# GpSimd's first eight row transfers of layer one, each behind a signal of TensorE

## The chip, the core and the metric

The kernel runs on one core of a Trainium2 chip. A core has TensorE (matrix products, written to PSUM), VectorE, ScalarE, GpSimd and SyncE, which run side by side and meet only at semaphores, and 16 DMA engines, which move data between HBM and the core's own memory. The metric is the device time of one execution in microseconds; less is better.

## The reference, cut to what matters

Three layers act on 4 sequences of 1,024 tokens with 128 features: a mixture of experts, a linear recurrence, and the same mixture of experts again. The two mixtures share their weights.

```python
x = x + 0.5 * ffn(layernorm(x))      # 8 experts, each token goes to 2 of them
x = x + lru(layernorm(x))            # complex diagonal recurrence along a sequence
x = x + 0.5 * ffn(layernorm(x))

def ffn(x):
    logits = x @ router_w.T + router_b
    topk_val, topk_idx = top_k(logits, 2)
    weights = softmax(topk_val)
    # every chosen expert: h1, h2 = split(x @ w1.T + b1); (silu(h1) * h2) @ w2.T + b2
    # the two results are summed with their weights
```

The reference computes all eight experts for all tokens and then picks. The kernel computes only what is picked.

## The kernel before, in words

**Routing.** A sequence g of a layer is 8 blocks of 128 tokens. VectorE and ScalarE normalise it, TensorE transposes it (`transpose_rows`, signal `s_tr`, one for each half) and multiplies it with the router's weights (`logits`, signal `s_logit`, one a sequence). VectorE picks the two best experts of each token (`choose`). TensorE then counts, by products with 0/1 matrices, how many tokens ahead of each chose the same expert (`rank`, signal `s_rank`, one a sequence), and from that VectorE makes the row of HBM to which each token goes (`slots`, signal `s_slot`). In the first layer the order of VectorE's work after the first sequence is written out by hand: slots of a sequence, the low half of a weight (`weight_low`), the low halves of the next sequence's rows (`row_parts`), `choose`, and so on.

**Rows.** GpSimd sends the tokens to their rows in HBM: `send_row(f, g, i)` is one indirect DMA of 128 rows, 16 of them for a sequence (8 blocks, two experts a token). In the first layer 42 of the 64 go ahead of all else on GpSimd (2 x 16 + `AHEAD_2`); the other 22 go two a tile within the first 11 tiles. The first of a sequence waits for `s_slot`, the ninth for `s_row`. In the kernel before, the seventh (`FIRST_PAUSE`) waits for the next sequence's logits too, and the thirteenth (`SECOND_PAUSE`) for its ranks.

**Experts.** The sorted rows are cut into 39 tiles of 256 rows (`NTILE`), each of one expert. When the last sequence's ranks and counts are there, VectorE makes a table of the tiles (`tile_table`), TensorE turns it into a row (`tile_row_of`, signal `s_listed`), and VectorE reads it back (`tile_list`, signal `s_tab`). SyncE then loads each tile, transposed, with its weights and biases (`load`). Tile 0 needs the 16 transfers of the first sequence, tile 1 those of the second, tile 9 of the third, tile 17 of the fourth (`FIRST_OF`, `s_sent`). TensorE starts on tile 0 when the weights of all eight experts are split into a high and a low half (`s_wl`); the last five splits stand behind `tile_list` on VectorE, and the loads of the experts 6 and 7 wait on SyncE for the splits of the experts 2 and 3, whose staging buffers they take. For a tile TensorE makes 24 products up (lines 1274 to 1276), and two tiles later two for the bias (line 1288) and 24 down (1294 to 1296). ScalarE and VectorE work between them. GpSimd scatters the two halves of each finished tile to HBM (`send_y`), and waits there for TensorE's products of three tiles on (`apart`).

The recurrence and the second mixture follow. The second layer's routing has pauses at the same two places.

Of the kernel before, what the change touches and what calls it, by code (L numbers as in the profile page):

```python
# [14 lines left out]
BATCH, SEQ = 4, 1024  # L15
# [21 lines left out]
STAGED = 4  # L37
AHEAD_2 = 10
FIRST_PAUSE, SECOND_PAUSE = 6, 12
APART = 3  # L40
LATE = BATCH - 1
RANKED, LISTED = 5, 10
# [12 lines left out]
def macaron_block(nc, x, nu_log, theta_log, b_re, b_im, c_re_t, c_im_t, d_vec, gamma_log,  # L55
                  router_t, router_b, w1_t, b1_t, w2_t, b2, out):
    ctx = ExitStack()
    with ctx:
# [3 lines left out]
        def sem(name):  # L62
            return ctx.enter_context(nc.semaphore(name))
# [133 lines left out]
        s_tr = sem("s_tr")  # L197
# [3 lines left out]
        s_logit = sem("s_logit")  # L201
# [4 lines left out]
        s_rank = sem("s_rank")  # L206
# [76 lines left out]
        def expert_tiles(f, tile):  # L283

            for t in range(NTILE):
                tile(t, lambda u: f * NTILE + t + u, lambda u, each: each * sent_before(f, t + u))
# [97 lines left out]
        @block.gpsimd  # L387
        def _(pool):
            pool.memset(ident[:, :], 0.0).then_inc(s_pool, 1)
            pool.memset(before[:, :], 1.0).then_inc(s_pool, 1)  # L390
            pool.iota(rev_i[:, 0:NE], pattern=[[-1, NE]], base=NE, channel_multiplier=0).then_inc(s_pool, 1)
            pool.iota(rev_i[:, NE:2 * NE], pattern=[[REG, NE]], base=0, channel_multiplier=0).then_inc(s_pool, 1)
            pool.iota(rev_i[:, 2 * NE:], pattern=[[1, 1]], base=0, channel_multiplier=1).then_inc(s_pool, 1)
            pool.iota(dest_i[:, :, :, :], pattern=[[TOK, TOPK], [SEQ, BATCH], [1, GT]], base=0,
                      channel_multiplier=GT).then_inc(s_pool, 1)
            pool.wait_ge(s_pool, 2)
            pool.affine_select(out=ident[:, :], in_=ident[:, :], compare_op=ALU.not_equal, fill=1.0, base=0,
                               pattern=[[-1, P]], channel_multiplier=1).then_inc(s_pool, 1)

            pool.affine_select(out=before[:, :], in_=before[:, :], compare_op=ALU.is_gt, fill=0.0, base=0,  # L400
                               pattern=[[1, P]], channel_multiplier=-1).then_inc(s_pool, 1)
            pool.memset(ones16[:, :], 1.0).then_inc(s_pool, 1)

            for m in range(TURNS):
                ins = pool.memset(double[:, m:m + 1], float(1 << m))
            ins.then_inc(s_pool, 1)

            def send_row(f, g, i):
                k, t = i // GT, i % GT
                if i == 0:  # L410
                    pool.wait_ge(s_slot, f * BATCH + g + 1)
                if i == GT:
                    pool.wait_ge(s_row, f * BATCH + g + 1)
                if i in (FIRST_PAUSE, SECOND_PAUSE) and g + 1 < (BATCH if f == 0 else LATE):

                    pool.wait_ge(s_logit if i == FIRST_PAUSE else s_rank, f * BATCH + g + 2)
                pool.indirect_dma_start(  # L417
                    out=rows_dram[f], out_offset=bass.IndirectOffsetOnAxis(ap=slot_i[:, k, f, g, t:t + 1], axis=0),
                    in_=rows[:, k, g, t, :], in_offset=None).then_inc(s_sent[g], 16)

            last_row = pool.to_reg(TOPK * TOK - 1)

            def apart(t, j, n):

                if t + APART < NTILE:
                    pool.wait_ge(s_up[j], n(APART + 1))

            def send_y(f, t, n):

                pool.wait_ge(s_yout, n(1))  # L430
                pool.sem_inc(s_ygo, 1)
                for r in range(2):
                    if r == 1:
                        apart(t, 0, n)
                    pool.indirect_dma_start(  # L435
                        out=y_dram[f],
                        out_offset=bass.IndirectOffsetOnAxis(ap=meta_i[:, t % METAS, r, 0:1], axis=0),
                        in_=yout[:, t % OUTS, r, :], in_offset=None, bounds_check=last_row,
                        oob_is_err=False).then_inc(s_ysent[t % OUTS], 16)

            for f in range(2):
                each = [(g, i) for g in range(BATCH) for i in range(TOPK * GT)]
                ahead = 2 * TOPK * GT + AHEAD_2
                for g, i in each[:ahead]:
                    send_row(f, g, i)
                later = iter(each[ahead:])

                def tile(t, n, dma):

                    send_y(f, t, n)  # L450
                    for j, (g, i) in enumerate(islice(later, 2 if f == 0 or t < 3 else BURSTS.get(t, 0))):
                        if j < 2:
                            apart(t, j + 1, n)
                        send_row(f, g, i)

                expert_tiles(f, tile)
# [933 lines left out]
```

## Time and profile before

| | us |
|---|---|
| median of 3 runs, no profiler | 562.7 (562.64 to 563.27) |
| profiled execution, first to last instruction | 662.6 |
| TensorE / VectorE / ScalarE / GpSimd busy in it | 481.3 / 425.0 / 350.1 / 284.6 |
| first product of tile 0, first product of tile 1 in it | 101.21, 105.60 |

The profile is one execution, with a record of every instruction. "Idle before <- X" in brackets is how long the engine had stood still before an instruction, and which one ended that. "Remote" and "issue" mean that the trace shows no instruction that ended it just then. The profiled execution shows no time of its own beside its span, and its span is 99.9 us above the median of the runs.

### The profile page before, as it was taken

What the parts mean: (1) busy time and instruction counts of PE and PEld (TensorE: products, weight loads), DVE (VectorE), ACT (ScalarE), POOL (GpSimd) and SP (SyncE); (2) the same over time, 40 slices, a digit from 0 to 9 for tenths busy, and PEclk for the clock granted to TensorE, in tenths of its full rate; (3) what the DMA queues carried; (4) which work ended last, traced back from release to release, by engine and by line L of the source; (5) the groups of instructions that cost most, each with busy time, mean ns of one, the idle gap of its engine ahead of it and who ended that gap; (6) DMA issues with size and microseconds to landing.
All of it is one profiled execution on the core that took longest, in us unless ns stands there. A gap on an engine that the chain in (4) does not pass through costs nothing.

```text
span 662.6 us, 15921 instructions
## 1 busy us (share of the span) xinstructions
PE 481.3 (73%) x4657; PEld 412.2 (62%) x4657; DVE 425.0 (64%) x1368; ACT 350.1 (53%) x797; POOL 284.6 (43%) x307
## 2 busy tenths in 40 slices
PE   7740008777699999998688777387945999999920
PEld 4530007556589899885587766266823998989920
DVE  8840387445478898772998772556823777767725
ACT  5871225445367777772506533075613677777820
POOL 1477600655655444453000574715465444444540
PEclk9555558987989999999697896679776999999975
DMA  8241132433223232204300111213222333333128
GB/s 288 73 145 48 48 104 43 89 84 74 66 58 73 63 57 59 63 27 142 114 0 1 34 46 36 65 34 76 54 78 77 71 68 68 60 62 61 46 72 309
DMA packets 94563, 50.27 MB, mean 76 GB/s; under 512 B 81902, under 2 KB 84720, under 8 KB 94484
## 3 DMA queue, kind: packets, MB, share of 16 engines
q1 hardware_dynamic: 85396, 32.31, 20.6%
q0 software_dynamic: 9088, 16.94, 8.1%
q8 instruction: 45, 0.74, 0.5%
q14 instruction: 34, 0.28, 0.2%
HBM read 17.25 MB, written 23.24 MB: 61 GB/s over the span
## 4 chain that ended last, share of the span: by engine, by line
PE 47%; issue 30%; DVE 9%; DMA 4%; ACT 4%; SPq 2%; another core or an unknown queue 1%; POOL 1%; POOLq 0%; DVEq 0%; ACTq 0%
PE bank L1276 10%; PE bank L1274 10%; PE bank L1275 10%; PE bank L1296 5%; PE bank L1294 5%; PE bank L1295 5%; DMA yin<-y 3%; PE bank L1288 1%; DVE w1l L825 1%; DVE xres L948 1%; ACT wst L551 1%; DVE wst L1063 1%; DVE bn L996 1%; ACT xn L472 1%
## 5 line engine op out<-in xcount | busy, mean ns | idle before, releaser
L435 POOL DMA_INDIRECT y<-yout,meta x156 | 154.0, 987 | 212.5 <-ACT yout L569 153.2
L1063 DVE SCALAR_TENSOR_TENSOR wst<-bank,bias,wst 128x256 f32<-128x256 f32 x312 | 146.5, 479 | 118.3 <-ACT wst L551 99.9
L1274 PE MATMUL bank<-xt_t,w1h 128*128 128x256 f16 x624 | 177.6, 285 | 27.2 <-DVE w2l L825 15.6
L417 POOL DMA_INDIRECT rows<-rows,slot_i x128 | 128.6, 1004 | 142.2 <-DVE slot_i L778 81.6
L551 ACT ACTIVATE wst<-bank,bias 128x256 f32<-128x256 f32 x312 | 141.5, 477 | 87.2 <-remote 64.2
L1276 PE MATMUL bank<-xt_t,w1l 128*128 128x256 f16 x624 | 177.3, 284 | 6.9 <-issue 6.9
L1275 PE MATMUL bank<-xt_t,w1h 128*128 128x256 f16 x624 | 177.4, 284 | 5.0 <-issue 5.0
L1294 PE MATMUL bank<-w2h,wst 128*128 x624 | 125.9, 224 | 8.1 <-issue 6.8
L1296 PE MATMUL bank<-w2h,wst 128*128 x624 | 124.0, 223 | 8.9 <-issue 8.8
L1295 PE MATMUL bank<-w2l,wst 128*128 x624 | 123.8, 223 | 6.9 <-issue 6.9
L1069 DVE TENSOR_TENSOR wst<-wst 128x512 f16<-128x512 f32 x156 | 107.6, 690 | 11.5 <-ACT wst L559 7.2
L559 ACT CAST wst<-wst 128x512 f16<-128x512 f32 x156 | 96.5, 619 | 29.2 <-DVE wst L1063 19.8
L1274 PEld LDWEIGHTS bank<-xt_t,w1h 128*128 x624 | 63.6, 102 | 35.3 <-issue 28.8
L1276 PEld LDWEIGHTS bank<-xt_t,w1l 128*128 x624 | 63.6, 102 | 18.8 <-issue 9.3
L1294 PEld LDWEIGHTS bank<-w2h,wst 128*128 128x128 f16 x624 | 62.2, 100 | 18.8 <-issue 14.5
L472 ACT ACTIVATE xn<-xres,shift,rstd 128x128 f32<-128x128 f32 x96 | 38.2, 481 | 64.3 <-DVE shift L711 42.1
L1275 PEld LDWEIGHTS bank<-xt_t,w1h 128*128 x624 | 63.5, 102 | 13.1 <-issue 8.0
L1295 PEld LDWEIGHTS bank<-w2l,wst 128*128 128x128 f16 x624 | 62.3, 100 | 11.3 <-issue 8.7
L1296 PEld LDWEIGHTS bank<-w2h,wst 128*128 128x128 f16 x624 | 62.4, 100 | 9.8 <-issue 9.6
L569 ACT ACTIVATE yout<-bank,meta 128x128 f32<-128x128 f32 x156 | 48.4, 363 | 28.3 <-remote 24.2
L948 DVE TENSOR_TENSOR xres<-xres,yin 128x1024 f32<-128x1024 f32 x16 | 19.6, 1224 | 27.8 <-DMA yin<-y 27.3
L1143 PE MATMUL bank<-ident,xn 128*128 128x128 f32 x96 | 20.3, 353 | 18.7 <-ACT xn L472 10.6
(205 smaller groups left out, 522.4 us busy)
## 6 DMA issues: line engine op xcount, KB each, us to landing
yin<-y SPq DMA_DIRECT2D x16, 512.0 KB, 4.6
wst<-in_w_t SPq DMA_DIRECT2D x8, 512.0 KB, 5.8
y<-yout,meta POOLq DMA_INDIRECT x156
rows<-padrow SPq DMA_DIRECT2D x18, 130.0 KB
xres<-in_x SPq DMA_DIRECT2D x8, 256.0 KB, 5.4
wst<-in_w_t SPq DMA_DIRECT2D x8, 256.0 KB, 6.8
rows<-rows,slot_i POOLq DMA_INDIRECT x128
out<-xres SPq DMA_DIRECT2D x4, 512.0 KB, 6.7
```

Of the source, the lines that this page charges most:

```text
L417: pool.indirect_dma_start(out=rows_dram[f], out_offset=bass.IndirectOffsetOnAxis(ap=slot_i[:, k, f, g, t:t + 1], axis=0), in_=rows[:, k, g ...
L435: pool.indirect_dma_start(out=y_dram[f], out_offset=bass.IndirectOffsetOnAxis(ap=meta_i[:, t % METAS, r, 0:1], axis=0), in_=yout[:, t % OU ...
L551: nc.scalar.activation(gate[:, j, :], up_ps[j][:, 0:SLOT], ACT.Silu, scale=1.0 / WS, bias=bias[:, t % STEP, j:j + 1]).then_inc(s_gate[j], 1)
L559: nc.scalar.copy(acth[:, t % BUFS, 2 * half:2 * half + 2, :], act[:, 2 * half:2 * half + 2, :]).then_inc(s_acth[half], 1)
L1063: V.scalar_tensor_tensor(act[:, j, :], up_ps[j][:, SLOT:], bias[:, t % STEP, HB + j:HB + j + 1], gate[:, j, :], ALU.add, ALU.mult).then_in ...
L1069: V.tensor_tensor(actl[:, t % BUFS, h2, :], act[:, h2, :], acth[:, t % BUFS, h2, :], ALU.subtract).then_inc(s_actl[half], 1)
L1274: T.matmul(o, w1h[:, bass.ds(at, P)], xt_t[:, t % STEP, 0, :], start=True, stop=False)
L1275: T.matmul(o, w1h[:, bass.ds(at, P)], xt_t[:, t % STEP, 1, :], start=False, stop=False)
L1276: ins = T.matmul(o, w1l[:, bass.ds(at, P)], xt_t[:, t % STEP, 0, :], start=False, stop=True)
L1294: T.matmul(o, acth[:, t % BUFS, c, rs], w2h[:, bass.ds(at, P)], start=False, stop=False)
L1295: T.matmul(o, acth[:, t % BUFS, c, rs], w2l[:, bass.ds(at, P)], start=False, stop=False)
L1296: ins = T.matmul(o, actl[:, t % BUFS, c, rs], w2h[:, bass.ds(at, P)], start=False, stop=(c == HB - 1 and r == 1))
```

## The change

In the first layer the pauses at the seventh and thirteenth transfer of a sequence go. In their place, transfers 1 to 8 of the first sequence (counted from 0) each wait for one further signal of TensorE, in the order in which it makes them: logits of sequence 1, transposes of 2, ranks of 1, logits of 2, transposes of 3, ranks of 2, logits of 3, ranks of 3. All later transfers of the first layer have only the waits for `s_slot` and `s_row`. The second layer keeps its two pauses.

```diff
+HELD = 8
...
-                if i in (FIRST_PAUSE, SECOND_PAUSE) and g + 1 < (BATCH if f == 0 else LATE):
+                if f == 0 and g == 0 and 0 < i <= HELD:
+
+                    turn, q = (i - 1) % 3, (i - 1) // 3
+                    if i == HELD:
+                        pool.wait_ge(s_rank, BATCH)
+                    elif turn == 0:
+                        pool.wait_ge(s_logit, q + 2)
+                    elif turn == 1:
+                        pool.wait_ge(s_tr, 2 * (q + 3))
+                    else:
+                        pool.wait_ge(s_rank, q + 2)
+                if f > 0 and i in (FIRST_PAUSE, SECOND_PAUSE) and g + 1 < LATE:
 
                     pool.wait_ge(s_logit if i == FIRST_PAUSE else s_rank, f * BATCH + g + 2)
```

## Rows read from the trace of the kernel before

**Rows 1.** The page's first line.
```profile
span 662.6 us, 15921 instructions
```

**Rows 2.** Windows, line 1288 alone (two products a tile): stretch, length, TensorE.
```profile
110.00:194.80 84.80, 4.02 (x27) 2.65 (x27) 0.90 0.33 73
203.00:292.00 89.00, 6.05 (x44) 4.02 (x44) 1.00 0.29 59
441.00:522.50 81.50, 3.47 (x23) 2.47 (x24) 0.81 0.28 68
```

**Rows 3.** Timeline of TensorE, routing and first tiles: start, length, operation.
```profile
41.77 3.56 PE L1156 MATMUL bank<-rwt,xnt 128*128 128x8 f32 x16
75.38 0.18 PE L1168 MATMUL bank<-seen,ones 128*128 128x32 f16 x1 [30.06 <-issue]
...
75.69 0.21 PE L1180 MATMUL bank<-seen,ones 128*128 128x64 f16 x1
...
101.21 0.39 PE L1274 MATMUL bank<-xt_t,w1h 128*128 128x256 f16 x1 [15.64 <-DVE w2l L825]
...
105.60 0.27 PE L1274 MATMUL bank<-xt_t,w1h 128*128 128x256 f16 x1
```

**Rows 4.** Timeline of VectorE, routing.
```profile
33.86 1.22 DVE L722 TENSOR_TENSOR rows<-xn,rows 128x1024 f16<-128x1024 f32 x1
37.96 0.23 DVE L737 TENSOR_TENSOR lg<-bank,rbb 128x64 f32<-128x64 f32 x1 [2.88 <-remote]
...
41.80 1.22 DVE L825 SCALAR_TENSOR_TENSOR w1l<-wst,w1h 128x1024 f16<-128x1024 f32 x1
...
48.72 0.23 DVE L768 TENSOR_TENSOR slotf<-bank,rev_f 128x64 f32<-128x64 f32 x1 [4.83 <-remote]
...
49.93 1.21 DVE L722 TENSOR_TENSOR rows<-xn,rows 128x1024 f16<-128x1024 f32 x1
71.35 0.23 DVE L737 TENSOR_TENSOR lg<-bank,rbb 128x64 f32<-128x64 f32 x1 [20.21 <-remote]
...
74.52 0.22 DVE L745 TENSOR_TENSOR oh<-oh 128x64 f16<-128x64 f32 x1
...
85.15 1.23 DVE L825 SCALAR_TENSOR_TENSOR w1l<-wst,w1h 128x1024 f16<-128x1024 f32 x1
```

**Rows 5.** Timeline of GpSimd: transfers 0, 8, 31 and 41.
```profile
24.22 1.86 POOL L417 DMA_INDIRECT rows<-rows,slot_i  x1 [21.55 <-DVE slot_i L778]
...
36.22 0.95 POOL L417 DMA_INDIRECT rows<-rows,slot_i  x1 [0.31 <-issue]
...
66.17 0.96 POOL L417 DMA_INDIRECT rows<-rows,slot_i  x1 [0.30 <-issue]
...
78.82 0.95 POOL L417 DMA_INDIRECT rows<-rows,slot_i  x1 [0.30 <-issue]
```

**Rows 6.** The chain of waits, last tiles: a scatter's issue and its landing.
```profile
637.69 0.98 POOL y L435
638.97 2.15 DMA y<-yout,meta
```

**Rows 7.** Timeline of SyncE and TensorE, second layer: tile 0's load, and its use.
```profile
419.04 1.27 SPq L344 DMA_TRANSPOSE xt_t<-rows  x1
...
422.18 0.39 PE L1274 MATMUL bank<-xt_t,w1h 128*128 128x256 f16 x1 [4.37 <-DMA xt_t<-rows]
```

**Rows 8.** Timeline of TensorE, second layer: tile 0's last products, tile 1's first.
```profile
426.73 0.27 PE L1276 MATMUL bank<-xt_t,w1l 128*128 128x256 f16 x1
432.29 1.11 PE L1143 MATMUL bank<-ident,xn 128*128 128x128 f32 x4 [5.29 <-issue]
...
435.17 0.42 PE L1275 MATMUL bank<-xt_t,w1h 128*128 128x256 f16 x1
```

**Rows 9.** Timeline of GpSimd, second layer: seventh transfer of a sequence, after its pause.
```profile
377.47 0.95 POOL L417 DMA_INDIRECT rows<-rows,slot_i  x1 [5.23 <-PE bank L1156]
```

**Rows 10.** Timeline of VectorE, second layer: the same signal, seen by VectorE.
```profile
377.22 0.23 DVE L737 TENSOR_TENSOR lg<-bank,rbb 128x64 f32<-128x64 f32 x1 [0.24 <-PE bank L1156]
```

## The prediction, made before the change was run

> **What bounds the kernel now.** I read the page first, for the span, and set it beside the median: the profiled execution takes 662.6 us [rows 1], the runs 562.7. So 99.9 us of the trace are not in the runs, and before a stall in it is priced one must ask whether the runs have it. Windows over the bias products come second, since they count tiles: in the quiet stretch of the first layer 22 tiles take 89.00 us, 4.05 each; in the stretch before it, where GpSimd makes four transfers a tile instead of two, 13.5 tiles take 84.80, which is 30.1 more than at 4.05; in the second layer 12 tiles take 81.50, 32.9 more [rows 2]. Most of each mixture is thus TensorE's own pace, and a start that is later or earlier by some us comes out at the end nearly one for one.
>
> The start is what the change touches, so the timelines of the routing are third. TensorE begins the last sequence's logits at 41.77 and is through at 45.33. VectorE, which waits for nothing else, takes them up at 71.35, after 20.21 idle, ended by "remote" [rows 3, 4]. It waited in the same way, for TensorE's signals, 2.88 before 37.96 and 4.83 before 48.72 [rows 4]. All that time GpSimd sends rows one after another [rows 5]. In the second layer, where GpSimd itself stands in a pause, a signal of the same kind ends VectorE's wait at 377.22 and GpSimd's at 377.47, both named after the product that gave it [rows 9, 10]. So in the trace TensorE's signals arrive late while GpSimd issues, and on time when it stands still. The three waits are 27.92 us of the start.
>
> **What the start would be without late signals.** The last ranks end at 75.69 + 0.21 = 75.90 [rows 3]; less the 27.92 that is **48.0**. The first product of tile 0 stands at 101.21 [rows 3]; less 27.92 that is 73.3. The tile table shrinks too: from the last pick (74.52) to the next weight split (85.15) VectorE takes 10.6 us for some 15 short links, while the pick, 14 such links, takes 74.52 - 71.35 = 3.2 [rows 4]. At that pace the table takes about 4.2, 6.4 less. TensorE could start at **66.9**. Tile 0's up products took 105.60 - 101.21 = 4.4 [rows 3], so tile 1 could start at 71.3 by the weights. Call D what of the late signals the runs do have: then it is 71.3 + D, with D = 34.3 in the trace.
>
> Tile 1 also needs transfer 31. It ends at 66.17 + 0.96 = 67.13 [rows 5]; a GpSimd scatter's landing ends 638.97 + 2.15 - 637.69 - 0.98 = 2.45 after its issue [rows 6]; a tile's load takes 422.18 - 419.04 = 3.14 until its first product [rows 7]. By the rows tile 1 can start at **72.7**. So tile 1 starts at the later of 72.7 and 71.3 + D. In the trace the second is far later (105.6) and the row transfers are hidden; without late signals the two are about level.
>
> **The change, part by part.**
>
> *The pauses taken away.* In the first layer they held nothing: the transfers stay at one per 1.265 us, which is (78.82 - 66.17) / 10, with 0.30 idle between them [rows 5]. Zero; the bounds are zero and some tenths, a register's worth of waiting each, under GpSimd's own 0.30.
>
> *The eight waits.* Seven of them end by the way, since the last ranks come after the signals that those wait for. The eighth decides: transfer 8, at 36.22 before [rows 5], cannot start until the last ranks, at 48.0 even when every signal is on time. That is **+11.8 us**, and behind it on GpSimd's queue stand transfers 9 to 41 and then the scatters of finished tiles, each moved by the same 11.8. Transfer 15, which tile 0 needs, ends at 48.0 + 7 x 1.265 + 0.96 = 57.8, lands at 60.3, and is loaded by 63.4: hidden behind the weights by 3.5 us, and if that cover went, tile 0 would wait. Transfer 31 is moved to 78.9 and tile 1 to **84.5**. Transfer 41 ends at 48.0 + 33 x 1.265 + 0.96 = 90.7; tile 0's scatter is due when tile 2 has its up products, some 6 us after 84.5, so it is hardly held. The 22 later transfers go with the scatters as before, 4 x 1.265 = 5.1 us a tile against 4.05 of TensorE, so that stretch gives nothing back.
>
> *TensorE's clock.* Between tile 0 (66.9 to 71.3, later by D) and tile 1 TensorE now stands still for up to 13 us. In the second layer it stood 5.29 us after tile 0 and its up products then took 0.42 again, after 0.27 [rows 8]. The lower level costs at most half of tile 0's 4.4, 2.2; below, nothing, if before pays it too. I take 1.5, nearer the top because the gap is longer than that of the row. Tile 1 counts as starting at 86.0.
>
> *What the waits buy.* When GpSimd stands still, signals arrive on time, so the held routing ends at 48.0 whatever D was. What they save is D, as far as it stood on the path.
>
> The change is then 86.0 less the later of 72.7 and 71.3 + D: +13.3 for D = 0, nothing at D = 14.7, and -19.6 with the trace's own 34.3.
>
> **How large D is in the runs.** In the trace's terms the start is late by 105.6 - 72.7 = 32.9, the busy stretches of the mixtures by 30.1 and 32.9: together 95.9. The runs lack 99.9. So nearly all of what the trace shows as late is missing from them, and if the second layer's routing has another 10 of it, about 10 are left for all places together. An even share leaves the start some 3; all of it at the start gives 10. I take D = 5, toward the middle because GpSimd is densest there. Change: 86.0 - 76.3 = **+9.7**, 562.7 + 9.7 = **572.4 us**. Its own range is D = 10 and no clock term (84.5 - 81.3 = +3.2) to D = 0 with all of it (86.7 - 72.7 = +14): 566 to 577. Against the profiled execution the same sum with its own D gives 662.6 - 19.6 = 643; I expect profile and runs to move in opposite directions.
>
> The Trainium skill bears on D (SBUF — State Buffer, section Who interferes with whom): TensorE never waits on another engine's use of the memory's ports. By that rule alone D would be 0 and the sum 576.0; the trace differs, its signals being late by up to 20.21 beside GpSimd's transfers [rows 4], and by it the sum would be 543. The page speaks of ports and not of signals, so it settles neither; the 572.4 does not use it.
>
> **Rivals.**
>
> *Faster: the signals are late in the runs as well.* The mechanism is the one above at its full size, at the start of layer one, where GpSimd issues 42 transfers with 0.30 between them. For it: it is in the trace, plainly, and the pauses of the second layer cure it there. Against it: 99.9 us that are not in the runs. It decides from D = 14.7; with D = 25 tile 1 was at 96.3 and comes to 86.0, so 562.7 - 10.3 = 552.4. Chance 0.28.
>
> *Slower still: the late signal moves on.* After 48.0 GpSimd sends 34 transfers freely, and the tile list's signal and tile 0's products fall beside them, where before they fell after 79.8, when it had stopped. The list's signal is queued ahead of five weight splits on VectorE. Were it late by 20.21, like the longest of before, TensorE would start at 87.1 and tile 1 at 91.5, with a warm clock: 91.5 - 76.3 = +15.2, 577.9. For it: nothing in the change pauses GpSimd there. Against: the same 99.9. Chance 0.10.
>
> *No change.* D is just about 14 and the later rows take up what the earlier list gives: 563. It needs a coincidence of two sums. Chance 0.06.
>
> **How the numbers follow.** The likeliest, 572.4, has 0.56; the other chances are as given. Slower by over 0.2% (1.1 us, about what a measurement of this kernel can tell from no change) is 0.56 + 0.10 = 0.66, within it 0.06, faster 0.28. A range of 552 to 578 leaves out the lower half of the faster case, a part of the slower rival and the upper edge of the likeliest, together near 0.2; the likeliest alone has 566 to 577.
>
> **What would show it.** Right: transfer 8 begins just after the last ranks, VectorE's three remote waits are gone or below 1 us, the last ranks end near 48, transfer 31 ends near 79, and tile 1's first product, not tile 0's, waits for its load at 84 or later. Wrong: transfer 8 earlier than 45 or later than 55 would break the +11.8; a late `s_listed`, seen as VectorE idle before `entry_i`, would be the third case; a median below 561.6 would show that the runs had D above 14.7, and that the subtraction of the two times, the weakest step, misled me.

## The result, and the profile after

The changed kernel takes 574.13 us (median of 4 runs, 572.33 to 575.82), the kernel before, run beside it, 562.99 (562.64 to 563.7). The ratio is 1.0196, its 95% interval 1.0165 to 1.0227: slower by 11.1 us, where +9.7 was forecast. (A ratio here is estimated from all the runs of both kernels, and can differ in the fourth place from the quotient of the two medians.)

The page's first line for the kernel after:

```profile
span 570.6 us, 15921 instructions
```

That is 3.5 us under the median of its runs, where the first trace of before stood 99.9 over its own [rows 1].

The timeline of GpSimd, kernel after: transfers 0, 7, 8, 16, 31 and 41.

```profile
24.18 1.85 POOL L429 DMA_INDIRECT rows<-rows,slot_i  x1 [21.51 <-DVE slot_i L790]
...
42.57 1.46 POOL L429 DMA_INDIRECT rows<-rows,slot_i  x1 [1.75 <-PE bank L1168]
48.45 0.96 POOL L429 DMA_INDIRECT rows<-rows,slot_i  x1 [4.42 <-PE bank L1192]
...
61.58 1.82 POOL L429 DMA_INDIRECT rows<-rows,slot_i  x1 [0.30 <-issue]
...
82.73 0.96 POOL L429 DMA_INDIRECT rows<-rows,slot_i  x1 [0.30 <-issue]
...
95.57 0.96 POOL L429 DMA_INDIRECT rows<-rows,slot_i  x1 [0.31 <-issue]
```

Against [rows 5], transfer 8 begins at 48.45 instead of 36.22, and what ended its wait is the product of the last ranks. Transfer 31 is at 82.73.

The timeline of TensorE, kernel after, which answers to [rows 3]:

```profile
38.73 3.56 PE L1168 MATMUL bank<-rwt,xnt 128*128 128x8 f32 x16
47.14 0.19 PE L1180 MATMUL bank<-seen,ones 128*128 128x32 f16 x1 [4.85 <-DVE seen L760]
...
47.44 0.21 PE L1192 MATMUL bank<-seen,ones 128*128 128x64 f16 x1
...
66.18 0.39 PE L1286 MATMUL bank<-xt_t,w1h 128*128 128x256 f16 x1 [15.71 <-DMA xt_t<-rows]
...
88.65 0.39 PE L1286 MATMUL bank<-xt_t,w1h 128*128 128x256 f16 x1 [18.24 <-DMA xt_t<-rows]
```

The ranks end at 47.65 (forecast 48.0), tile 0 starts at 66.18 (forecast 66.9, later by D), and then TensorE stands for 18.24 us until tile 1's rows are loaded.

The timeline of VectorE, kernel after, the places of [rows 4]:

```profile
34.96 0.22 DVE L749 TENSOR_TENSOR lg<-bank,rbb 128x64 f32<-128x64 f32 x1
...
40.78 0.22 DVE L780 TENSOR_TENSOR slotf<-bank,rev_f 128x64 f32<-128x64 f32 x1
...
43.12 0.21 DVE L749 TENSOR_TENSOR lg<-bank,rbb 128x64 f32<-128x64 f32 x1
...
46.27 0.22 DVE L757 TENSOR_TENSOR oh<-oh 128x64 f16<-128x64 f32 x1
...
50.05 1.23 DVE L837 SCALAR_TENSOR_TENSOR w1l<-wst,w1h 128x1024 f16<-128x1024 f32 x1
```

The three "remote" waits are gone, and the table from the pick to the next weight split takes 3.8 us instead of 10.6. Taken alone this is the trace of a cure. The first experiment shows that there was nothing to cure.

### The profile page after: what moved, and what is told of

Read it like the earlier page. It is cut to its first block, busy times and chain, and to the rows that moved or that the text cites. A ratio compares the mean times of both kernels' runs of the same rounds, so it can differ in the third digit from the quotient of the medians.

```text
span 570.6 us, 15921 instructions
## 1 busy us (share of the span) xinstructions
PE 449.6 (79%) x4657; PEld 394.9 (69%) x4657; DVE 424.1 (74%) x1368; ACT 358.1 (63%) x797; POOL 299.8 (53%) x307
## 4 chain that ended last, share of the span: by engine, by line
SPq 27%; PE 20%; DVE 17%; issue 12%; POOL 12%; DMA 8%; ACT 3%; POOLq 0%; ACTq 0%; DVEq 0%
SPq L345 10%; POOL rows L429 10%; SPq L355 4%; SPq L349 4%; PE bank L1286 4%; PE bank L1288 4%; PE bank L1287 4%; SPq L352 3%; SPq L336 3%; DMA yin<-y 3%; DMA xt_t<-rows 2%; DVE wst L1075 2%; PE bank L1307 2%; PE bank L1306 2%; PE bank L1308 2%
## 5 line engine op out<-in xcount | busy, mean ns | idle before, releaser
L447 POOL DMA_INDIRECT y<-yout,meta x156 | 161.2, 1033 | 116.3 <-ACT yout L581 81.5
L1286 PE MATMUL bank<-xt_t,w1h 128*128 128x256 f16 x624 | 173.6, 278 | 53.2 <-DMA xt_t<-rows 53.2
L429 POOL DMA_INDIRECT rows<-rows,slot_i x128 | 136.6, 1067 | 130.6 <-DVE slot_i L790 80.6
L563 ACT ACTIVATE wst<-bank,bias 128x256 f32<-128x256 f32 x312 | 145.3, 473 | 84.4 <-PE bank L1288 49.3
L1287 PE MATMUL bank<-xt_t,w1h 128*128 128x256 f16 x624 | 173.3, 278 | 0.0
L1288 PE MATMUL bank<-xt_t,w1l 128*128 128x256 f16 x624 | 173.0, 277 | 0.0
L1306 PE MATMUL bank<-w2h,wst 128*128 x624 | 122.8, 220 | 0.8 <-DVE wst L1081 0.7
L1308 PE MATMUL bank<-w2h,wst 128*128 x624 | 120.7, 220 | 0.0
L1307 PE MATMUL bank<-w2l,wst 128*128 x624 | 120.5, 220 | 0.0
L1286 PEld LDWEIGHTS bank<-xt_t,w1h 128*128 x624 | 62.1, 100 | 62.8 <-issue 57.2
L1306 PEld LDWEIGHTS bank<-w2h,wst 128*128 128x128 f16 x624 | 61.0, 98 | 7.6 <-issue 4.3
L1287 PEld LDWEIGHTS bank<-xt_t,w1h 128*128 x624 | 62.1, 100 | 4.5
L1308 PEld LDWEIGHTS bank<-w2h,wst 128*128 128x128 f16 x624 | 61.1, 98 | 0.0
L1155 PE MATMUL bank<-ident,xn 128*128 128x128 f32 x96 | 18.2, 330 | 10.6 <-ACT xn L484 10.4
```

The lines of the kernel that those rows point to most:

```text
L429: pool.indirect_dma_start(out=rows_dram[f], out_offset=bass.IndirectOffsetOnAxis(ap=slot_i[:, k, f, g, t:t + 1], axis=0), in_=rows[:, k, g ...
L447: pool.indirect_dma_start(out=y_dram[f], out_offset=bass.IndirectOffsetOnAxis(ap=meta_i[:, t % METAS, r, 0:1], axis=0), in_=yout[:, t % OU ...
L563: nc.scalar.activation(gate[:, j, :], up_ps[j][:, 0:SLOT], ACT.Silu, scale=1.0 / WS, bias=bias[:, t % STEP, j:j + 1]).then_inc(s_gate[j], 1)
L1286: T.matmul(o, w1h[:, bass.ds(at, P)], xt_t[:, t % STEP, 0, :], start=True, stop=False)
L1287: T.matmul(o, w1h[:, bass.ds(at, P)], xt_t[:, t % STEP, 1, :], start=False, stop=False)
L1288: ins = T.matmul(o, w1l[:, bass.ds(at, P)], xt_t[:, t % STEP, 0, :], start=False, stop=True)
```

## The experiments

Lines of GpSimd, VectorE and TensorE below keep the operation and the tiles; line numbers move with each edit.

**e1, the kernel before, profiled again.** No edit.

> The kernel before, unchanged, profiled a second time. If the late signals of the first trace belonged to that one execution: a span near 561, the four logits signals within 0.1 us of their products, transfer 8 near 36, the last ranks near 48, tile 0's first product near 66.5 and tile 1's near 77 (11 before the changed kernel's 88.65). If the late signals belong to this kernel whenever it is profiled: a span near 660, VectorE again idle for some 20 us before the last pick, and tile 1 near 105.

Its time is 565.88 us. The page's first line:

```profile
span 564.1 us, 15921 instructions
```

The timeline of TensorE:

```profile
38.77 3.56 PE L1156 MATMUL bank<-rwt,xnt 128*128 128x8 f32 x16
47.48 0.19 PE L1168 MATMUL bank<-seen,ones 128*128 128x32 f16 x1 [5.15 <-DVE seen L748]
...
66.57 0.39 PE L1274 MATMUL bank<-xt_t,w1h 128*128 128x256 f16 x1 [15.70 <-DVE w2l L825]
...
77.35 0.39 PE L1274 MATMUL bank<-xt_t,w1h 128*128 128x256 f16 x1 [5.92 <-DMA xt_t<-rows]
```

The timeline of VectorE, the last pick's first link:

```profile
43.40 0.22 DVE L737 TENSOR_TENSOR lg<-bank,rbb 128x64 f32<-128x64 f32 x1
```

The timeline of GpSimd: transfers 8, 13, 22, 24, 27 and 31.

```profile
36.22 0.96 POOL L417 DMA_INDIRECT rows<-rows,slot_i  x1 [0.30 <-issue]
...
42.54 1.77 POOL L417 DMA_INDIRECT rows<-rows,slot_i  x1 [0.30 <-issue]
...
55.33 2.09 POOL L417 DMA_INDIRECT rows<-rows,slot_i  x1 [0.30 <-issue]
...
59.85 1.82 POOL L417 DMA_INDIRECT rows<-rows,slot_i  x1 [0.30 <-issue]
...
66.22 0.96 POOL L417 DMA_INDIRECT rows<-rows,slot_i  x1 [0.30 <-issue]
...
71.27 0.96 POOL L417 DMA_INDIRECT rows<-rows,slot_i  x1 [0.30 <-issue]
```

The same kernel, with GpSimd sending without a stop, and no signal is late: the logits that end at 42.33 are not even waited for, since VectorE comes to them at 43.40. The trace's records of the four logits signals stand within 0.02 us of the ends of their products; in the first trace the last two stood 4.2 and 26.0 us behind them. This execution took 565.88 us, more than any of the 13 timed ones of before on the same chip (559.4 to 565.35), so none of those has room for a late start either: D is 0. The late signals of the first trace belong to that one execution and not to the kernel. Tile 1 starts at 77.35, after an idle of 5.92 that its load ends: the row transfers bound it already before the change. From here on "before" means this trace.

**e2, the last wait alone.**

```diff
-                if f == 0 and g == 0 and 0 < i <= HELD:
-                    ... (the seven other waits)
+                if f == 0 and g == 0 and i == HELD:
+
+                    pool.wait_ge(s_rank, BATCH)
```

> Of the eight waits only the last stays (transfer 8 waits for the last ranks); transfers 1 to 7 run freely and the old pauses stay away. If the whole cost is that transfer 8 starts at 48 instead of 36: as the changed kernel, 574 (+11 on before), tile 1 again near 88.6. If the seven stops before it carry part of the cost: 566 to 570.

573.61 us against 562.42 for before on the same chip, ratio 1.0199 (1.0157 to 1.0241). GpSimd's transfer 8 and TensorE's tile 1:

```profile
49.14 0.95 POOL L421 DMA_INDIRECT rows<-rows,slot_i  x1 [12.56 <-PE bank L1184]
```

```profile
89.28 0.39 PE L1278 MATMUL bank<-xt_t,w1h 128*128 128x256 f16 x1 [17.99 <-DMA xt_t<-rows]
```

One wait of 12.56 us does what the eight did together. (The whole trace lies some 0.7 us later than that of the changed kernel, from transfer 0 at 24.88 on.) Beside the eighth wait the seven others add nothing: without them transfers 1 to 7 go earlier, and transfer 8 then stands before the same gate.

**e3, no pause in the first layer.** The block of the eight waits is taken out and nothing put in.

> No pause at all in the first layer: the old ones removed and none put in. If the runs have no late signals and the old pauses held nothing: 563, within 0.2% of before. If freely running transfers hold TensorE's signals back in the runs too: slower than before, by some us up to 20.

562.71 against 562.42, ratio 0.9997 (0.997 to 1.0024). Transfer 8 starts at 36.25 and tile 1 at 77.66. The old pauses held nothing, and in this kernel free transfers hold no signal back.

**e4, a longer hold.**

```diff
                     if i == HELD:
                         pool.wait_ge(s_rank, BATCH)
+                        pool.wait_ge(s_wl, 2 * 3)
```

> The changed kernel, with transfer 8 waiting for the third expert's weight split as well, which ends at 52.07 in its trace: transfer 8 starts near 52.5 instead of 48.45, 4 us later. If tile 1 waits for the rows and each us of hold is a us at the end: 578 (+15 on before), tile 1 near 92.7. If something else had bound tile 1 at 88.65: 574.

579.17 against 562.42, ratio 1.0318 (1.0272 to 1.0363). GpSimd's transfer 8, and TensorE's tile 0 and tile 1:

```profile
52.82 1.63 POOL L430 DMA_INDIRECT rows<-rows,slot_i  x1 [8.84 <-DVE w2l L838]
```

```profile
73.01 0.39 PE L1287 MATMUL bank<-xt_t,w1h 128*128 128x256 f16 x1 [22.61 <-DMA xt_t<-rows]
...
93.33 0.39 PE L1287 MATMUL bank<-xt_t,w1h 128*128 128x256 f16 x1 [15.74 <-DMA xt_t<-rows]
```

4.37 us more of hold than in the changed kernel are 4.68 at tile 1 and, against before, 16.8 at the end instead of 11.1. Tile 0 is late now too, since transfer 15 has lost its cover, but tile 1 still comes later.

**e5, seven waits without the last.** `0 < i <= HELD` becomes `0 < i < HELD`.

> The changed kernel without its last wait: transfers 1 to 7 wait as in it, transfer 8 follows freely after transfer 7, which waits for the last logits. If each us of hold is a us at the end: transfer 8 starts near 44.3 (42.57 + 1.46 + 0.30 in the changed kernel's trace), 4.1 earlier than with the eighth wait, tile 1 near 84.5, 570 (+7.5 on before). If the eighth wait alone makes the cost: 563.

569.25 against 561.9, ratio 1.0135 (1.0092 to 1.0178). Transfer 8 and tile 1:

```profile
44.37 0.96 POOL L429 DMA_INDIRECT rows<-rows,slot_i  x1 [0.30 <-issue]
```

```profile
84.74 0.39 PE L1286 MATMUL bank<-xt_t,w1h 128*128 128x256 f16 x1 [14.08 <-DMA xt_t<-rows]
```

So the seven are not free by themselves. Without the eighth, the last of them holds transfer 7 until the last logits and with it transfer 8 until 44.37, and that costs 7.4. The last gate in front of transfer 8 sets the price.

**e6, the last wait further back.** `g == 0` becomes `g == 1` in e2's condition: transfer 24 waits for the last ranks.

> The changed kernel's last wait (for the last ranks) is put before transfer 24 instead of 8, and the other seven are gone. Transfer 24 stands at 59.9 without pauses, after the ranks at 48. If the cost is the place and not the wait: 563, transfer 24 near 59.9 and tile 1 near 77.5. If waiting for the ranks costs wherever it stands: 566 or more.

561.84 against 561.9, ratio 1.0007 (0.9984 to 1.0031). Transfer 24 does not stand still:

```profile
60.32 1.82 POOL L421 DMA_INDIRECT rows<-rows,slot_i  x1 [0.31 <-issue]
```

The ranks, at 48, are long there, and tile 1 starts at 77.45. The wait is free where GpSimd arrives after what it waits for.

The five holds in one table (us; the last column is the difference of medians on the same chip):

| | transfer 8 starts | tile 1 starts | median | to before |
|---|---|---|---|---|
| e3, none | 36.25 | 77.66 | 562.71 | +0.3 |
| e5, to the last logits | 44.37 | 84.74 | 569.25 | +7.4 |
| changed kernel, to the last ranks | 48.45 | 88.65 | 574.13 | +11.1 |
| e2, the last wait alone | 49.14 | 89.28 | 573.61 | +11.2 |
| e4, to a weight split | 52.82 | 93.33 | 579.17 | +16.8 |

From first to last row transfer 8 moves by 16.57, tile 1 by 15.67 and the median by 16.5: nearly one for one.

**e7, all rows of the first layer first.** If the rows bind, moving them up should gain.

```diff
-                ahead = 2 * TOPK * GT + AHEAD_2
+                ahead = BATCH * TOPK * GT if f == 0 else 2 * TOPK * GT + AHEAD_2
```

> No pauses in the first layer, and all 64 of its row transfers ahead of GpSimd's scatters instead of 42, so that no tile has four transfers. If GpSimd's rows set both tile 1 (77.5) and the pace of tiles 2 to 15 (16 us over 4.07 a tile in e1's trace, for four transfers a tile take 5.1): tile 1 stays near 77.5, tiles follow at 4.07 from there, 548 to 553 (10 to 14 below before). If the scatters, now later, hold up TensorE through the eight output buffers: 563 or more, with gaps from tile 8 on.

562.1 against 561.9, ratio 1.0007 (0.9978 to 1.0035): no gain, and neither theory was right. The last of the 64 transfers ends at 115 instead of 148, TensorE is not held up by the scatters, yet the tiles after tile 3 still come some 5 us apart. The timeline of SyncE, e7, shows why:

```profile
81.68 1.25 SPq L345 DMA_TRANSPOSE xt_t<-rows  x1
...
85.51 1.24 SPq L345 DMA_TRANSPOSE xt_t<-rows  x1
...
89.39 0.40 SPq L325 DMA_DIRECT2D rows<-padrow  x1
89.83 0.93 SPq L329 DMA_DIRECT2D rows<-padrow  x1
91.46 1.23 SPq L345 DMA_TRANSPOSE xt_t<-rows  x1
...
95.34 0.35 SPq L325 DMA_DIRECT2D rows<-padrow  x1
96.39 1.23 SPq L345 DMA_TRANSPOSE xt_t<-rows  x1
```

A tile's load follows the last after 4.9 to 6 us where a transfer of padding rows stands between, after 3.8 to 4.2 ahead of the first of them, and 3.8 to 4.8 behind the last. SyncE's queue, then, and not GpSimd's four transfers, would pace these tiles; e9 and e10 try it.

**e8, e7 with the eight waits.**

> As e7, but with the changed kernel's eight waits. If the hold costs what tile 1 loses, with nothing given back later: 11 to 12 above e7, tile 1 near 88.6. If the tight stretch behind tile 1 took part of the cost in the changed kernel (there +11.5 at tile 1 were +9 at the last tile), nothing is given back here and the cost is the full 11.5 to 12.

571.94 against 561.9, ratio 1.0193 (1.0151 to 1.0236), 9.8 above e7. Tile 1 starts at 88.19, in e7 at 77.04: 11.15 there. That the whole 11.5 would reach the end is not borne out; the runs of e7 spread over 5 us, so whether something is given back stays open.

**e9, e7 with the padding moved.** SyncE issues the nine padding transfers of the first layer right after tile 0's load.

```diff
+                    if f == 0 and t == 0:
+                        for e in range(NE):
+                            pad(e)
+                        pad_end()
-                    first_pad = STEP if f == 0 else KNOWN - NE
-                    if first_pad <= t < first_pad + NE:
+                    first_pad = KNOWN - NE
+                    if f > 0 and first_pad <= t < first_pad + NE:
                         pad(t - first_pad)
-                    if t == STEP:
+                    if f > 0 and t == STEP:
                         pad_end()
```

> e7 (no pauses in the first layer, its 64 row transfers ahead of the scatters), with SyncE's nine transfers of padding rows moved from the loads of tiles 4 to 11 to the time between the loads of tiles 0 and 1, where SyncE stands still for 11 us in e7. If the pace of tiles 3 to 12 is SyncE's (its loads come 5.0 apart with a padding transfer between, 4.0 without): those tiles at 4.07, 8 to 10 below e7, 552 to 554, with tile 1 unmoved near 77.5. If the pace is something else's: 562 as e7.

552.81 against 562.63, ratio 0.9834 (0.9792 to 0.9875): 9.8 us faster than before, as no other version is. Windows over the bias products, e9: 24 products, 12 tiles, in 49.3 us.

```profile
86.50:135.80 49.30, 3.31 (x24) 2.35 (x24) 1.00 0.44 83
```

In e7 the same window holds 22, 11 tiles:

```profile
86.50:135.80 49.30, 2.92 (x22) 1.60 (x21) 1.00 0.41 103
```

The timeline of SyncE, e9:

```profile
63.40 8.83 SPq L325 DMA_DIRECT2D rows<-padrow  x8
72.28 0.43 SPq L329 DMA_DIRECT2D rows<-padrow  x1
74.61 1.26 SPq L345 DMA_TRANSPOSE xt_t<-rows  x1
...
78.57 1.24 SPq L345 DMA_TRANSPOSE xt_t<-rows  x1
```

The padding goes into the time in which SyncE had waited for tile 1's rows; tile 1 comes at 78.25.

**e10, the padding moved, without the rows first.** e9's edit on e3.

> The same move of the padding transfers, without sending the rows first: 42 row transfers ahead, two a tile after that. If SyncE sets the pace of tiles 3 to 12 and GpSimd the time of transfer 63 (148 in e1's trace, and tile 17 needs it): tiles 3 to 12 at 4.07, then a stall at tile 17 of 8 to 11 us, 560 to 563. If GpSimd's four transfers a tile matter for nothing: 553 as e9.

565.2 against 562.63, ratio 1.0059 (1.0025 to 1.0092). The window of e9 over the bias products, and TensorE at tile 17, e10:

```profile
86.50:135.80 49.30, 3.30 (x24) 2.34 (x24) 1.00 0.42 80
```

```profile
154.12 0.39 PE L1279 MATMUL bank<-xt_t,w1h 128*128 128x256 f16 x1 [8.43 <-DMA xt_t<-rows]
```

With four transfers a tile on GpSimd again, but no padding between SyncE's loads, 12 tiles take the 49.3 us as in e9: the pace was SyncE's. The stall forecast is there, 8.43 us at tile 17 for the rows of transfer 63, which ends at 149.5. In e1 tile 17 starts at 154.31, after a wait of 2.01, so all that the quicker tiles had gained is gone at this one wait. The time is 2 us above its range. Part of that is TensorE's clock: behind the longer wait the granted clock was 0.64 from 154.1 to 158.4, a mix of the lower level (1.2 GHz) and the full one (2.4 GHz), where e1 had 1.00, and TensorE made 34 products there against 48. By e1's pace that is an estimated 1.3 us; the rest stays open. So e7's edit alone gains nothing, the padding's alone costs 2.6, and the two together gain 9.8: behind SyncE's pace stood GpSimd's last row.

## Why the prediction came out

**The hold, +11.8: right.** Transfer 8 moved by 12.2 (36.22 in e1 to 48.45), transfer 31 by 11.46, tile 1 by 11.30, the median by 11.1. e2 shows that the eighth wait is enough for it, e5 that an earlier last gate costs less, e6 that the wait costs by its place, and the table that each us of hold is about a us at the end.

**D = 5: wrong, it is 0.** The subtraction of the two times pointed the right way, but the step "an even share ... all of it" left D a value because some us could not be placed. Its sum was off as well: 95.9 and another 10, less the 99.9, leave 6.0 and not "about 10". In e1 no signal is late, and with D = 0 the formula would have said +13.3.

**The clock, +1.5: mis-sized, it is 0.3.** Tile 1 starts at the lower level after a wait of 5.92 in e1 as after 18.24 in the changed kernel: the granted clock is 0.50 (1.2 GHz) from 77.3 to 81.0 in e1 and from 88.6 to 92.9 in the changed kernel, over 18 and 21 of tile 1's products. From tile 1's first product to the first bias product, 30 products later, it is 5.09 and 5.42 us. Before paid nearly the same. The two sizes were off in opposite ways: the forecast was 11.8 for the hold, 1.5 more for the clock and 3.6 less for D (76.3 less 72.7); without the last two it is 11.8, and 11.3 was measured at tile 1. That the total of +9.7 came so near 11.1 is thus in part luck, since one wrong term took back some of the other.

**When transfer 31 is through: mis-sized in both kernels, so without effect.** The prediction had tile 1 at 72.7 before and 84.5 after; they are 77.35 and 88.65. The transfers beside the weight splits take up to 2.09 us instead of 0.96, and those splits fell after the transfers in the trace that was read [rows 4, 5]. In e1 transfer 31 ends 5.1 us later than the prediction had it, at 72.23. A row's landing was taken at 2.45 after its issue's end; the chain of waits after says 1.3:

```profile
82.73 2.27 DMA rows<-rows,slot_i
85.11 1.23 SPq L345
```

From 82.73 the landing takes 2.27, of which 0.96 are the issue; the load follows at 85.11 and tile 1 at 88.65, 3.54 behind it, where 3.14 was taken. For the same reason the cover of 3.5 us that tile 0 was given is gone: transfer 15 ends at 61.27 instead of 57.8, and tile 0's wait in the changed kernel is ended by its load and no longer by the last weight split. It costs nothing there (66.18, in e1 66.57); in e4 it does.

**"That stretch gives nothing back": about right, its ground wrong.** Behind tile 1 the prediction held GpSimd's four transfers a tile (5.1 us) against TensorE's 4.05. e7 takes them away and the tiles come no faster; e10 leaves them and takes SyncE's padding away, and 12 tiles take 49.3 us. SyncE's loads, some 5 us apart, set the pace. That "the table takes about 4.2" does not follow from the pace that was taken for it either: 15 links, at 14 in 3.2 us, are 3.4. It took 3.8, and with D at 0 tile 1's time does not rest on it.

**Profile and runs in opposite directions: right in sign, wrong in its ground.** The span fell from 662.6 to 570.6, not to 643. The sum gave the fall to the waits, which were to bring the signals in. e1 falls to 564.1 without them, and e3, with no pause in the first layer, to 561.3 as its profile has it. That signals "arrive late while GpSimd issues, and on time when it stands still" was read from one execution; e1, e3 and e7 refute it as a rule of this kernel. That trace itself held lines against it. VectorE, kernel before, first trace:

```profile
26.00 0.22 DVE L737 TENSOR_TENSOR lg<-bank,rbb 128x64 f32<-128x64 f32 x1 [0.95 <-PE bank L1156]
...
84.65 0.19 DVE L807 TENSOR_REDUCE at_tile<-reached 128x1 f32<-128x33 f32 x1 [1.07 <-DVE reached L805]
```

At 26.00 the signal is on time, though GpSimd had been sending since 24.22 [rows 5]; at 84.65 VectorE is held up behind an instruction of its own, though GpSimd's last transfer ahead of the tiles had ended at 79.77. That trace also holds only 5,980 records of semaphore updates, the eleven others 11,318 to 11,563. So this execution, or its recording, was unlike the others as a whole. What made the signals late in it stays open: no other one shown here has it, so it could not be tried.

**The rivals.** *Late signals in the runs*: refuted by e1, e3 and the timed runs. *The late signal moves on to the tile list*: the list is read at 51.99, right behind the split, with GpSimd sending freely; refuted. *No change*: it needed D near 14.

## What to carry to other kernels

Set a trace's span beside the timed median before a stall in it is priced; where they lie far apart, profile the same kernel again before anything else. In this kernel a wait put into a queue costs what it moves the last transfer that someone waits for, and it is free where the queue arrives after the signal (e6). Where one queue bounds a stretch and another the tile behind it, easing one gains nothing until the other is eased too (e7, e10, e9).

## What the runs showed of the hardware

GpSimd's indirect transfers were longer while VectorE made its last five weight splits. In e1 the transfers at 55.33 to 64.09 took 2.09, 1.82, 1.82, 1.82 and 1.82 us, those from 66.22 to 78.85 0.96 again. VectorE's five splits ran from 55.38 to 65.88, e1:

```profile
55.38 1.20 DVE L825 SCALAR_TENSOR_TENSOR w1l<-wst,w1h 128x1024 f16<-128x1024 f32 x1
...
65.19 0.69 DVE L825 SCALAR_TENSOR_TENSOR w2l<-wst,w2h 128x512 f16<-128x512 f32 x1
```

That is some 4.6 us on the path to tile 1. The holds move the transfers and leave the splits about where they are, and the long ones are then others: 22 to 26 in e1, 16 to 20 in e5, 13 to 17 in the changed kernel, 9 to 13 in e4. So the length goes with the time and not with the transfer. Not every overlap shows it: in e1 transfer 10, begun at 38.75, took 0.96 beside the split from 38.87 to 40.08. The Trainium skill (SBUF — State Buffer, section Who interferes with whom) says that a VectorE instruction with two inputs in SBUF contends with a GpSimd instruction that reads SBUF. If an indirect transfer counts as such an instruction, the five long transfers of e1 agree with that and transfer 10 does not show it. That the splits cause it was not tried by an edit.
